# Attention scores of the second query half on 32-row tiles, two heads side by side in two PSUM banks, around those of the first half

## What is computed

```python
q = (x @ Wq).reshape(b, t, KV, G, D)      # KV = 4, G = 4, D = 32
k = (x @ Wk).reshape(b, t, KV, D)
scores = jnp.einsum('bqhgd,bkhd->bhgqk', q, k) * scale
scores = jnp.where(causal_mask, scores, -jnp.inf)
w = jax.nn.softmax(scores, axis=-1)
y = jnp.einsum('bhgqk,bkhd->bqhgd', w, v)
y = y.reshape(b, t, H * D)
return y @ Wo
```

## Time and profile before

| | us |
|---|---|
| median of 3 runs (lowest, highest) | 1992.71 (1992.0, 1996.39) |
| the profiled execution: time | 1994.85 |
| the profiled execution: span of the core | 1992.8 |
| TensorE busy | 1866.1 (94% of the span) |
| mean granted TensorE clock | 0.979 of full speed |

### The profile page before, as it was taken

One profiled execution on the slowest core, in us unless ns is written; L12 is line 12 of the kernel. 1 busy time (PEld: TensorE's weight loads), 2 busy tenths in 40 slices (PEclk: granted clock), 3 DMA queues, 4 the chain that ended last, 5 costly groups with the idle time before them and its releaser, 6 DMA issues.

```text
span 1992.8 us, 33389 instructions
## 1 busy us (share of the span) xinstructions
PE 1866.1 (94%) x12784; PEld 1490.7 (75%) x12784; DVE 1143.3 (57%) x1852; ACT 688.5 (35%) x1501; POOL 262.8 (13%) x239
## 2 busy tenths in 40 slices
PE   5999996699996899999999999999999999999997
PEld 4777775578885577777777878777777778787776
DVE  4555554567775445555464565564755655655665
ACT  5556654211211323333332232332422322424321
POOL 2334434233432000000000000000000000000000
PEclk9999998799998899999999999999999999999999
DMA  2011001200000201112020030020120300300011
GB/s 90 22 32 32 21 21 45 89 23 11 21 0 1 90 1 56 45 27 79 11 75 17 13 83 13 6 89 6 39 56 13 83 13 6 88 7 10 9 48 43
DMA packets 38912, 71.51 MB, mean 36 GB/s; under 512 B 7233, under 2 KB 15553, under 8 KB 38081
## 3 DMA queue, kind: packets, MB, share of 16 engines
q1 hardware_dynamic: 38848, 70.63, 11.6%
HBM read 64.85 MB, written 5.77 MB: 35 GB/s over the span
## 4 chain that ended last, share of the span: by engine, by line
PE 57%; DVE 6%; issue 2%; ACT 1%; DVEq 0%; POOLq 0%; POOL 0%
PE pair L1682 10%; PE pair L1684 10%; PE pair L1683 10%; PE y_ps L1682 3%; PE y_ps L1684 3%; PE y_ps L1683 3%; PE pair L1804 2%; PE pair L1805 2%; PE qa_ps L1682 2%; PE qa_ps L1684 2%; PE qa_ps L1683 2%; PE qd_ps L1858 1%; PE qd_ps L1859 1%; PE qa_ps L1696 1%; PE qd_ps L1682 1%
## 5 line engine op out<-in xcount | busy, mean ns | idle before, releaser
L1682 PE MATMUL pair<-XH,GUH 128*128 128x512 f32 (+1 forms) x960 | 376.2, 392 | 0.0
L1684 PE MATMUL pair<-XH,GUL 128*128 128x512 f32 (+1 forms) x960 | 375.4, 391 | 0.0
L1683 PE MATMUL pair<-XL,GUH 128*128 128x512 f32 (+1 forms) x960 | 374.6, 390 | 0.0
L1596 DVE TENSOR_TENSOR h<-pair,sg 128x512 f32<-128x512 f32 (+1 forms) x120 | 82.7, 689 | 382.2 <-ACT sg L1368 382.1
L1368 ACT ACTIVATE sg<-pair 128x512 f32<-128x512 f32 (+1 forms) x120 | 71.6, 596 | 502.5 <-PE pair L1805 406.6
L1684 PEld LDWEIGHTS pair<-XH,GUL 128*128 128x128 f32 (+1 forms) x960 | 171.7, 179 | 47.9
L1683 PEld LDWEIGHTS pair<-XL,GUH 128*128 128x128 f32 (+1 forms) x960 | 171.9, 179 | 47.0
L1682 PEld LDWEIGHTS pair<-XH,GUH 128*128 128x128 f32 (+1 forms) x960 | 171.6, 179 | 47.0
L1270 POOL TENSOR_TENSOR qb_raw<-qb_raw,qb_scale 128x704 f32<-128x704 f32 x8 | 13.9, 1733 | 1039.9 <-DMA qb_scale<-in_gu_scale 1039.9
L1418 DVE TENSOR_TENSOR HL<-h,HH 128x512 fp32r<-128x512 f32 (+1 forms) x120 | 82.9, 691 | 83.7 <-ACT HH L1280 83.7
L264 ACT ACTIVATE p<-s_ps,nm 128x128 f32<-128x128 f32 (+1 forms) x256 | 103.6, 427 | 76.5 <-DVE nm L347 76.5
(11 more groups left out here) (302 smaller groups left out, 4075.6 us busy)
## 6 DMA issues: line engine op xcount, KB each, us to landing
gu_raw<-in_gu SPq DMA_DIRECT2D x20, 512.0 KB, 4.3
wrep<-soft_f SPq DMA_DIRECT2D x64, 128.0 KB
dw_raw<-in_dw SPq DMA_DIRECT2D x10, 512.0 KB, 4.0
xT_raw<-in_xT SPq DMA_DIRECT2D x8, 512.0 KB, 3.8
x_raw<-in_x SPq DMA_DIRECT2D x8, 512.0 KB, 3.6
c_raw<-in_cT SPq DMA_DIRECT2D x8, 512.0 KB, 4.2
out<-xtok SPq DMA_DIRECT2D x4, 1024.0 KB, 4.2
gu_raw<-in_gu SPq DMA_DIRECT2D x10, 384.0 KB, 3.1
```

Of the source, the lines that this page charges most:

```text
L1596: nc.vector.tensor_tensor(h[0:M, b, :], pair[b][1][0:M, :], sg[0:M, b, :], ALU.mult).then_inc(h_rdy, 1)
L1682: mm(out, wh, xh, start=first, stop=False)
L1683: mm(out, wh, xl, start=False, stop=False)
L1684: return mm(out, wl, xh, start=False, stop=last)
```

## The change

Units 1 and 2 are no longer computed with 128 rows and the zeros in `KH`/`KL`. Each head has its own matmuls of 32 rows and 256 columns, three per head. They are issued in pairs, one head in bank 1 and one in bank 2: heads 0 and 2 first (`late(0)`), then heads 1 and 3 (`late(1)`), with the whole of unit 0 between the two. The masks of units 1 and 2 come last. Since `late(0)` comes first, TensorE waits for the exponentials of all three units of group g-1 ahead of it. Two matmuls in one bank from different row tiles must not meet, so `late(1)` waits until `late(0)` is done (`half_done`).

```diff
-                for unit, i, kv, keys, m in ((0, 0, slice(0, 4), slice(0, P), mask0), (1, 1, slice(0, 2), slice(0, S), mask1),
-                                             (2, 1, slice(2, 4), slice(0, S), mask1)):
-                    if g >= 1:
-                        pe.wait_ge(exp_done, U * (G * b + g - 1) + unit + 1)
-                    elif unit == 0:
-                        pe.wait_ge(lo_rdy, (G + 1) * (b + 1))
-                    q = slice(i * P, (i + 1) * P)
-                    out = s_ps[unit][:].rearrange("p (v s) -> p v s", v=4 if unit == 0 else 2)
-                    three(out, QH[:, g, q], QL[:, g, q], KH[:, kv, keys], KL[:, kv, keys], True, False)
-                    mm(out, identR[:], m[:], start=False, stop=True).then_inc(s_done, 1)
+                def late(first_kv):
+
+                    alone(pe, past)
+                    for n, (Q, K) in enumerate(((QH, KH), (QL, KH), (QH, KL))):
+                        for kv in (first_kv, first_kv + 2):
+                            rows = slice(HD * kv, HD * kv + HD)
+                            done = mm(s_ps[1 + kv // 2][:, kv % 2 * S:(kv % 2 + 1) * S], Q[rows, g, P:S], K[rows, kv, :],
+                                      start=n == 0 and first_kv == 0, stop=False, skip_group_check=True)
+                            if first_kv == 0 and n == 2:
+                                done.then_inc(half_done, 1)
+
+                if g >= 1:
+                    pe.wait_ge(exp_done, U * (G * b + g - 1) + U)
+                else:
+                    pe.wait_ge(lo_rdy, (G + 1) * (b + 1))
+                late(0)
+                out = s_ps[0][:].rearrange("p (v s) -> p v s", v=4)
+                three(out, QH[:, g, 0:P], QL[:, g, 0:P], KH[:, :, 0:P], KL[:, :, 0:P], True, False)
+                mm(out, identR[:], mask0[:], start=False, stop=True).then_inc(s_done, 1)
+                pe.wait_ge(half_done, 2 * (G * b + g + 1))
+                late(1)
+                for unit in (1, 2):
+                    mm(s_ps[unit][:].rearrange("p (v s) -> p v s", v=2), identR[:], mask1[:], start=False, stop=True,
+                       skip_group_check=True).then_inc(s_done, 1)
```

More of the change, by code:

```diff
@@ L164, in attention @@
             sem(n) for n in ("wo_done", "r_rdy", "ve_rdy", "rstd_rdy", "xs_rdy", "xt_done", "xt_act", "xt_dve", "xtok_rdy"))
-        dve_steps = sem("dve_steps")
+        dve_steps, half_done = sem("dve_steps"), sem("half_done")
         NPJ = G + 2
```

## The result

| | us |
|---|---|
| after, median of 4 runs (lowest, highest) | 2040.69 (2037.29, 2042.73) |
| before, median of 4 runs | 1992.36 |
| ratio with its 95% interval | 1.0239 (1.0217 to 1.0262) |
| forecast (range) | 2010.3 (2000.5 to 2021.5) |

What follows compares the result with a forecast made beforehand. The prediction took the first attention's chain of waits, with an xT load without slack, as the bound, though TensorE is 94% busy. Seven batches (16.5 us) plus 1.1 for the last, 17.6, on 1992.7 gave 2010.3 us (2000.5 to 2021.5).

Steps and rivals of the forecast that it cites:

- What a call costs: Scores call, first attention: six pairs at 0.13 us, unit 0, masks and switches make 2.72 us against 2.73, nothing gained.
- D: Length of a new call of scores: forecast 2.72 us, between 2.08 and 3.38 at its ends.
- entering and leaving: Switches around each block of 32-row tiles in scores: 0.09 us for entering, 0.20 for leaving; the low end is nothing.
- Rivals 2 and 3: 2: pairs run one after the other, 2018.6 us, chance 0.16; 3: free switches, pairs 0.12, 2002.6 us, chance 0.12.
- The moved wait: All of exps(g-1) must be read before scores(g); TensorE idles about 2 us ahead of scores(1) and scores(3).
- D + h - 2.11: Loss per batch with the load: call length plus time to its first ready bank (h, 1.75 us) less 2.11: 2.36 us.
- The load: The xT load in the first attention has no slack: read 3.9 us after issue, a later `vals` delays exps(2).
- The clock: Rival 5: waits of 2 us drop the granted clock from 2.4 to 1.2 GHz, 16 us more, 2026 us, chance 0.07.
- A rule against it: Loads overlap running matmuls only in different row groups; by it a pair in scores would approach twice 0.12 us.

Runs made afterwards that it cites:

- the filled kernel: The changed kernel with eight wide matmuls of 512 columns into a free bank ahead of the wait in scores(1) and scores(3): 2011.99 us, ratio 1.0110.
- moved wait alone: The kernel before, wide matmuls and old order kept, with one wait for all three units of exponentials ahead of a call of scores: 2005.91 us, ratio 1.0074.
- wide pairs: The changed kernel, same order and waits, but each small matmul takes all 128 rows, so no 32-row tiles: 2026.53 us, ratio 1.0185.

## Why the prediction was wrong

Point by point, by its own steps:

- **What a call costs: right.** D was forecast 2.72 and came out 2.68. Pairs are 0.11 to 0.12 from the second of a block on (taken: 0.13), so the two ends of entering and leaving are worth about what I took. Rivals 2 and 3 are out.
- **The moved wait: right in the middle batches, short at the two ends.** Idle 2.00 us ahead of scores(1) (1.9 forecast) and 1.97 ahead of scores(3) (2), seven waits for xT. With the wide matmuls the formula D + h - 2.11 gave 1.8 us and 1.8 was measured; with the tiles 2.36, and the filled kernel showed 2.5. Filled, the changed kernel takes 2012.0 us, where the forecast said 2010.3; by its ratio of 1.0110 it loses 22 us where 17.6 were worked out. In its profile the six middle batches lose 2.3 to 2.7 us each, but the first loses 3.9 (worked out: 2.4) and the last 4.4 (1.1), in which the one fall left stands. What makes up the first batch's excess is open.
- **The load: right**, and shown by itself: 21 us for 2.9 us of delay in seven batches.
- **The clock: the step that failed.** In the rivals I wrote that "1.36 us of waiting leave the clock at 1.00" and gave the fall a chance of 0.07 and a price of 2 us per batch. It happened in every batch, mostly twice. A fall lasted some 7 us in ten of the 14 and some 3 in the others. One of 7 us cost 2.4 to 2.8 us of its batch (44.0 to 44.4 with one, 47.0 with two, against 41.65 filled). Of the missing part of the sum, 48 - 18 = 30 us, this one term is 26 by the two ratios, 29 by the medians. It was put at nothing in the forecast and left out of the range, and the rival's 16 us were too few: 8 stretches of 4 us, where there were 14 falls and 82 us.
- The flaw in the argument was to read the 1.36 us as an allowance for idle time beside any work. That row stood beside wide matmuls. The change set tiles, which use a quarter of the rows each, right behind idle times that were half as long again. The table shows both sides, with the two longest idle times of a middle batch:

| kernel | scores | idle times in a batch, us | falls | us at 1.2 GHz |
|---|---|---|---|---|
| before | wide | 1.4, 0.7 | 0 | 0 |
| before, V projection first | wide | 1.7, 0.7 | 0 | 0 |
| before, late load | wide | 1.4, 1.5 to 1.7 | 0 | 0 |
| moved wait alone | wide | 1.9, 2.0 to 2.2 | 3 | 14 |
| wide pairs | wide | 1.9, 1.8 to 2.2 | 8 | 34 |
| wide pairs, both filled | wide | 0.7, 0.6 | 1 | 3 |
| changed, both filled | tiles | 0.6 | 1 | 7 |
| changed, unit 0 first | tiles | 0.8, 0.7 | 6 | 20 |
| changed, V projection first | tiles | 1.3, 0.8 | 4 | 17 |
| changed, filled ahead of scores(1) | tiles | 2.0 to 2.2 | 8 | 48 |
| changed, filled ahead of scores(3) | tiles | 2.0, 0.6 | 9 | 65 |
| changed | tiles | 2.0, 1.6 to 2.1 | 14 | 82 |

Shown is that filling the idle times removes 13 of the 14 falls and 26 to 29 us. With the same idle times wide matmuls had 8 falls and less than half the time at 1.2 GHz, in one profiled execution of each. Argued only is that tiles count for less, and why. Open is what decides in the rows between, where the clock falls in one batch and holds in the next with the same idle times to 0.1 us.

- **A rule against it.** The rule of the Trainium skill that I weighed ("TensorE: Matmul & The Clock Gate", What overlaps and what doesn't), read as a load that would not pass its own row group's matmul, would have given pairs of twice the length. The trace of the kernel after shows 0.11 us from pair to pair, although each pair uses the row groups of the pair before it: here such loads cost nothing beside the matmuls. Rule and measurement differ in this reading, and the measurement decides.

## What to carry to other kernels

Where work is moved behind a later wait, follow every queue that hangs on the end of that work: here a transfer with 1.4 us of visible waiting in the whole first attention turned a late projection into a late batch. Count each new idle time of TensorE twice, once for itself and once for the clock: here one of 2 us cost another 1.5 to 2.8 us where the clock fell, and beside small tiles it nearly always fell. Work that does no good, put into the idle time, gave back 26 to 29 of 48 us. And price the entering and leaving of a tiling mode before the gain from it: two blocks per call ate nearly all of 0.65 us of saved streaming (2.68 us a call against 2.73).

## What the runs showed of the hardware that I had not expected

- The granted clock of the changed kernel fell when TensorE was busy again: at 127.9 us, 1.0 us after the idle time had ended at 126.87. It then stayed at 0.50 through more than 6 us of unbroken work. With the moved wait alone one fall began inside the idle time (75.8 us, idle until 76.4).
- Two 32-row matmuls with loads of 128 columns each, in two banks, cost together what one costs (0.11 to 0.12 us), from the second pair of a block on; from the first pair to the second it was 0.19 to 0.23 us.
- In the last batch TensorE idles ahead of `values`. In the seven kernels in which this was 2.05 to 2.10 us, the two with wide pairs among them, a fall followed; in the five in which it was 1.46 to 1.76 us, none did. That the length decides is not shown.
